# A hybrid block on one Trainium2 core: the band of the local first scores by a TensorE product instead of by VectorE

## The chip, the cores and the metric

The kernel is one program on one core of a Trainium2 chip. Time is device microseconds (us) from launch to end on that core. Before the change three runs gave 568.0, 569.43 and 571.01 us; the median is 569.43 us.

## The reference, cut to what matters

Input is 4 sequences of 512 tokens with 128 channels. Four layers follow each other, each with a layer norm ahead of it and a residual sum behind it: a Haar wavelet mixing ("a"), a mixture of 8 experts with 2 chosen, an attention ("c"), and the same mixture again. The change lies in the attention, of 16 heads with 8 channels:

```
attn = einsum('bhnd,bhmd->bhnm', q, k) * scale
band = abs(idx[:, None] - idx[None, :]) <= 128
local_out  = softmax(where(band, attn, -inf)) @ v
topk_out   = softmax(q . k of the 128 chosen tokens) @ their v
global_out = softmax(q . k of the first 64 tokens) @ their v
out = (local_out + topk_out + global_out) / 3
```

Each of the three softmaxes needs its own maximum for each query. The local one is taken over the band alone: a query block of 128 sees its own key block and half of each neighbour, cut along a diagonal.

## The kernel before, in words

The attention works in 16 groups (NG), each of 4 heads of one sequence. Scores are computed twice. The first scores (`p1`, TensorE) lie with queries on partitions and serve only to find the maxima (`maximum`, VectorE, called DVE below); the maxima are written beside the queries (QST), transposed with them (`transpose_again`), and so are subtracted within the second product. The second scores (`p2`, TensorE) lie with keys on partitions, ScalarE (ACT) takes their exponential into PT (line 1117), and `pv` (TensorE, lines 1935, 1938, 1941) multiplies it by the values.

A group has 22 first-score units (UNITS_Q): for each of 4 heads 4 local ones, a query block each, over 2 key blocks at the edges (256 columns) or 3 in the middle (384 columns); 4 "top" ones over the 128 chosen keys (line 1889), and 2 "global" ones for head pairs (line 1892), both of 512 columns. A local unit is one float16 matmul (line 1884). DVE then runs one instruction that adds the float32 mask BANDQ (0 or -1e30) to the scores, writes the sum to a scratch tile (JUNK, which is XN_a or XN_c) and takes the maximum (line 1460); the trace shows it as CUSTOM_DVE_ANT_0 and a short DVE_READ_ACCUMULATOR2_ANT. The first scores go round 3 PSUM banks: unit v waits until the maximum of unit v-3 is done (`max_done`).

The second scores have 22 units (UNITS) too. Their mask is already a product: TensorE multiplies the identity IDB by the bfloat16 mask BANDK into the bank (lines 1907 and 1910), and the score matmul adds to it (line 1912).

The order is fixed. TensorE's loop goes over groups g and second-score units u; beside each it does the first-score units that `scored_beside` gives, of the group after the next in time (LEAD is 8 units ahead), and at fixed u other work: `transpose_qk` of group g+2 at u=0, `gather_kv` of g+2 at u=13 (lines 1861, 1865: chosen keys and values by one-hot products), `transpose_again` at u=20, and parts of the mixture. The order of the units within a group is `q_order`: globals at places 2 and 5, tops at 8, 11, 14, 17.

Keys reach the matmuls over SyncE's DMA queue (SP). `spread` copies the local keys of a group from KALL to a set of zero-padded tiles (lines 552 and 554, six transfers, the last on line 554) behind ACT's copies on lines 960 and 963; TensorE waits for them (`keys_in`) at the group's first unit. `spread_top` copies the chosen keys (line 560, four transfers) behind DVE's lines 1442 and 1443; TensorE waits for them (`top_keys_in`) at the group's first top unit. The key tiles are of three sets that take turns: KZB, KZC, and the set QS, VS, PR, HXT.

Ahead of the loop stands a prologue (148 to 170 us) that computes the first scores of group 0 and four units of group 1 between the tail of the early mixture (lines 1346, 1347) and the choice of the top tokens.

Of the kernel before, what the change touches and what calls it, by code (L numbers as in the profile page):

```python
# [20 lines left out]
ALU = mybir.AluOpType  # L21
# [3 lines left out]
P = 128  # L25
B, L, D = 4, 512, 128
T = L // P
# [21 lines left out]
GPAIR = 2  # L49
UNITS_Q = HG * (T + 1) + HG // GPAIR  # L50
GLOBAL_W, TOP_W = HG * T, HG * T + HG // GPAIR
UNITS = HG * T + HG + HG // 2
# [26 lines left out]
def key_range(t):  # L79

    return max(t - 1, 0), min(t + 1, T - 1) + 1


def q_order():

    local = [divmod(w, T) for w in range(GLOBAL_W)]
    order = {w: (GPAIR * n, T + 1) for n, w in enumerate((2, 5))} | {w: (i, T) for i, w in enumerate((8, 11, 14, 17))}
    return [order[w] if w in order else local.pop(0) for w in range(UNITS_Q)]


def q_unit(g, w):

    if g >= 2:
        return Q_ORDER[w]
    if w < GLOBAL_W:
        return divmod(w, T)
    if w < TOP_W:
        return GPAIR * (w - GLOBAL_W), T + 1
    return w - TOP_W, T
# [161 lines left out]
def build(nc, x, w_qv, w_out, haar, haar_inv, chan, rows, w_gate, w1, w2, w_qkv, w_s, w_o,  # L261
          ident, band_q, band_k, tri, iota, tie, kshift, out):
    ctx = ExitStack()
    with ctx:
# [87 lines left out]
        VSEL = [sb(f"VSEL{n}", [P, HG, SLOT]) for n in range(3)]  # L352
        JUNK = [XN[n][:, :, :].rearrange("p t d -> p (t d)") for n in "ac"]
        PT = [sb(f"PT{n}", [P, L]) for n in range(PT_RING)]
# [831 lines left out]
        def _(dve):  # L1186
# [260 lines left out]
            def maximum(g, w):  # L1447
# [5 lines left out]
                dve.wait_ge(S["p1_done"], v + 1)  # L1453
                if t < T:
                    lo, hi = key_range(t)
                    n, off = (hi - lo) * P, (lo - t + 1) * P
                    if v >= 2:

                        dve.wait_ge(S["max_done"], v - 1)
                    nc.vector.tensor_tensor_reduce(  # L1460
                        out=JUNK[v % 2][:, 0:n], in0=P1_BANK[v % SCORE_RING][:, 0:n], in1=BANDQ[:, off:off + n],
                        scale=1.0, scalar=OFF, op0=ALU.add, op1=ALU.max,
                        accum_out=qst[:, t, h, SHIFT + LOCAL:SHIFT + LOCAL + 1]).then_inc(S["max_done"], 1)
                elif t == T:
# [200 lines left out]
        def _(pe):  # L1665
# [203 lines left out]
            def p1(g, w):  # L1869
# [8 lines left out]
                if t < T:  # L1878
                    if w == 0:

                        pe.wait_ge(S["misc_free"], free("qk", g) + 1)
                        pe.wait_ge(KEYS_IN[g % 2], spread_done(g))
                    lo, hi = key_range(t)
                    last = mm(bank[:, 0:(hi - lo) * P], q[:, t * P:(t + 1) * P], k[:, lo * P:hi * P], start=True, stop=True)  # L1884
                elif t == T:
# [346 lines left out]
```

## Time and profile before

| | us |
|---|---|
| median of three runs | 569.43 |
| span of the profiled execution, first to last instruction | 567.5 |
| TensorE (PE) busy | 497.0 |
| DVE busy | 390.0 |
| ScalarE (ACT) busy | 350.9 |
| GpSimd (POOL) busy | 311.3 |
| loop over the groups | about 170 to 485 |

The profile gives the profiled execution's span, not its launch time; the median lies 1.9 us above that span. PE's busy time counts overlapping matmuls once but includes the drain of each, so that it overstates how full the array is. Neighbouring starts tell what an instruction really costs its engine when it doesn't wait.

### The profile page before, as it was taken

The numbers are of one execution on the slowest core, as the hardware profiler recorded it, in microseconds if no ns is written. First come the engines' busy times: TensorE is split into PE (matmuls) and PEld (weight loads), VectorE is DVE, ScalarE is ACT, GpSimd is POOL, SyncE is SP. The second block draws the span as 40 slices with busy tenths as digits, with TensorE's granted clock in tenths as the row PEclk, the third lists the DMA queues.
The fourth block names the chain that finished last, engine by engine and source line by source line (L and its number), as shares of the span: only waits on it lengthen the run. The fifth ranks groups of instructions, "written<-read, shape, count | busy, mean of one in ns | idle before, by whom it ended". The sixth has DMA issues, their size and how long they took to land.

```text
span 567.5 us, 13117 instructions
## 1 busy us (share of the span) xinstructions
PE 497.0 (88%) x4267; PEld 307.3 (54%) x4267; DVE 390.0 (69%) x1400; ACT 350.9 (62%) x835; POOL 311.3 (55%) x464
## 2 busy tenths in 40 slices
PE   7999899886767999999899989899987878789886
PEld 4477676676434445545455545445544422668664
DVE  4777876468886698899878897777975650235325
ACT  6587555786208676667567668566664455567653
POOL 3411165456499976493199967897075051354340
PEclk9999999998989999999999999999999697999999
DMA  7996011764210000000000000010001005356506
GB/s 229 360 362 228 2 42 56 255 206 156 64 29 14 3 14 14 14 4 15 12 9 9 15 12 14 27 30 20 12 4 45 12 34 183 125 183 195 163 15 185
DMA packets 47539, 47.78 MB, mean 84 GB/s; under 512 B 10323, under 2 KB 39129, under 8 KB 47472
## 3 DMA queue, kind: packets, MB, share of 16 engines
q1 hardware_dynamic: 44464, 41.37, 23.2%
q0 software_dynamic: 3008, 5.58, 3.1%
q8 instruction: 34, 0.56, 0.4%
q14 instruction: 33, 0.27, 0.1%
HBM read 11.32 MB, written 19.48 MB: 54 GB/s over the span
## 4 chain that ended last, share of the span: by engine, by line
PE 58%; DVE 17%; issue 9%; ACT 7%; DMA 3%; POOL 3%; another core or an unknown queue 2%; SPq 1%; DVEq 0%; ACTq 0%; POOLq 0%
PE BANK L1836 5%; PE BANK L1935 5%; PE BANK L1912 4%; PE BANK L1804 4%; PE BANK L1792 4%; PE BANK L1884 4%; PE BANK L2022 4%; PE BANK L1941 2%; PE BANK L1938 2%; PE BANK L2160 2%; PE BANK L1741 2%; PE BANK L1907 2%; POOL OH L725 2%; DVE XN_c L1460 2%
## 5 line engine op out<-in xcount | busy, mean ns | idle before, releaser
L1117 ACT ACTIVATE PT<-BANK 128x256 f32<-128x256 f32 (+2 forms) x352 | 158.1, 493 | 108.5 <-PE BANK L1912 75.1
L725 POOL TENSOR_SCALAR OH<-IOTA,POS 128x128 bf16<-128x128 bf16 x240 | 140.1, 604 | 4.3 <-DVE OH L1580 3.2
L1460 DVE CUSTOM_DVE_ANT_0 XN_a<-BANK,BANDQ 128x256 f32<-128x256 f32 (+1 forms) x128 | 56.7, 443 | 25.6 <-PE BANK L1884 15.6
L1460 DVE CUSTOM_DVE_ANT_0 XN_c<-BANK,BANDQ 128x384 f32<-128x384 f32 (+1 forms) x128 | 67.9, 530 | 9.3 <-PE BANK L1884 5.5
L733 POOL TENSOR_TENSOR SUM<-NRM 128x128 f32<-128x128 f32 x16 | 7.3, 456 | 104.5 <-DVE NRM L1481 104.5
L1465 DVE TENSOR_REDUCE QST<-BANK 128x4 f16<-128x512 f32 x64 | 44.2, 694 | 16.8 <-PE BANK L1889 12.7
L1935 PE MATMUL BANK<-PT,V 128*32 128x256 f32 (+1 forms) x512 | 49.1, 456 | 0.7 <-issue 0.3
L757 POOL DMA_INDIRECT yt_late<-QKV,IDY_late x31 | 30.4, 979 | 32.7 <-DVE QKV L1338 25.2
L1836 PE MATMUL BANK<-XNT_ALL,W 128*128 128x512 f32 x96 | 45.3, 596 | 0.0
L934 ACT ACTIVATE PT<-BANK 128x512 f32<-128x512 f32 x48 | 27.6, 598 | 22.3 <-PE BANK L1836 20.4
L1907 PE MATMUL BANK<-BANDK,IDB 128*128 128x256 bf16 x128 | 36.0, 282 | 5.7 <-issue 3.5
L2022 PEld LDWEIGHTS BANK<-W,PT 128*128 128x128 f32 x256 | 30.8, 192 | 7.4 <-issue 5.7
L757 POOL DMA_INDIRECT yt_early<-QKV,IDY_early x23 | 22.6, 981 | 19.2 <-ACT QKV L990 10.6
L2022 PE MATMUL BANK<-W,PT 128*128 128x128 f32 x256 | 31.5, 276 | 0.7 <-ACT PT L941 0.7
L1910 PE MATMUL BANK<-BANDK,IDB 128*128 128x128 bf16 x128 | 28.6, 225 | 3.9 <-ACT PT L1117 2.1
L1910 PEld LDWEIGHTS BANK<-BANDK,IDB 128*128 128x128 bf16 x128 | 12.5, 98 | 34.7 <-ACT PT L1117 13.9
L746 POOL DMA_INDIRECT xs_late<-QKV,IDX x24 | 23.8, 990 | 7.9 <-issue 7.1
L970 ACT COPY QKV<-BANK 128x128 f32<-128x128 f32 x54 | 14.1, 260 | 19.3 <-PE BANK L1783 11.3
L1468 DVE TENSOR_REDUCE QST<-BANK 128x8 f16<-128x512 f32 x32 | 22.2, 695 | 5.2 <-remote 3.2
L1323 DVE TENSOR_SCALAR IDY_late<-QKV 128x1 uint32<-128x1 f32 x31 | 4.7, 151 | 29.2 <-PE BANK L1804 17.8
L1884 PE MATMUL BANK<-KZC,QT 128*128 128x256 f16 (+1 forms) x80 | 23.8, 300 | 1.0 <-DVE QST L1460 0.9
L1884 PE MATMUL BANK<-KZB,QT 128*128 128x256 f16 (+1 forms) x80 | 23.5, 300 | 1.2 <-DVE QST L1460 1.1
(363 smaller groups left out, 1286.6 us busy)
## 6 DMA issues: line engine op xcount, KB each, us to landing
xs_late<-W SPq DMA_DIRECT2D x1, 6984.0 KB, 38.4
xs_early<-W SPq DMA_DIRECT2D x1, 4680.0 KB, 19.6
KZB<-W SPq DMA_DIRECT2D x16, 256.0 KB
KZC<-W SPq DMA_DIRECT2D x15, 256.0 KB
PT<-W SPq DMA_DIRECT2D x11, 256.0 KB
QKV<-xs_late SPq DMA_DIRECT2D x31, 72.0 KB
W<-w SPq DMA_DIRECT2D x2, 1024.0 KB, 8.5
QKV<-xs_early SPq DMA_DIRECT2D x23, 72.0 KB
```

The lines of the kernel that those rows point to most:

```text
L725: last = nc.gpsimd.tensor_scalar(OH[g % 2][:, i, t, :], IOTA[:, :], POS[:, t, c:c + 1], None, ALU.is_equal)
L757: nc.gpsimd.indirect_dma_start(YT[w.tag][:, :], bass.IndirectOffsetOnAxis(ap=IDY[w.tag][:, i:i + 1], axis=0), YST[w.tag][slot], None, boun ...
L934: nc.scalar.activation(RELU[u % 4][:, :], UP_BANK[hh][:, :], ACT.Relu).then_inc(s["relu"], 1)
L1117: nc.scalar.activation(PT[u % PT_RING][:, 0:w], P2_BANK[u % SCORE_RING][:, 0:w], ACT.Exp, scale=SCALE).then_inc(S["exp_done"], 1)
L1460: nc.vector.tensor_tensor_reduce(out=JUNK[v % 2][:, 0:n], in0=P1_BANK[v % SCORE_RING][:, 0:n], in1=BANDQ[:, off:off + n], scale=1.0, scala ...
L1465: nc.vector.reduce_max(qst[:, :, h, SHIFT + TOP], P1_BANK[v % SCORE_RING][:, :].rearrange("p (t s) -> p t s", t=T), AX_X).then_inc(S["max_ ...
L1836: mm(UP_BANK[hh][:, :], W1[:, e, hh * P:(hh + 1) * P], XNT_ALL[:, cols(b)], start=True, stop=True).then_inc(s["up"], 1)
L1884: last = mm(bank[:, 0:(hi - lo) * P], q[:, t * P:(t + 1) * P], k[:, lo * P:hi * P], start=True, stop=True)
L1907: mm(edges, IDB[:, :], BANDK[:, :, :], start=True, stop=False, skip_group_check=True)
L1910: mm(bank[:, (q - lo) * P:(q - lo + 1) * P], IDB[:, :], BANDK[:, side, :], start=True, stop=False, skip_group_check=True)
L1935: last = mm(out_n[:, lo * P:hi * P], V32[par][:, r, h, :], pt[:, 0:(hi - lo) * P], start=(r == 0), stop=False, skip_group_check=True)
L2022: last = mm(DOWN_BANK[n % 2][:, t * P:(t + 1) * P], HID_T[n % 2][hh][:, t * P:(t + 1) * P], W2[:, e, hh, :], start=(hh == 0), stop=(hh == ...
```

## The change

Four things change in the attention's first scores.

A local unit first multiplies IDB by both halves of BANDK (256 columns) into the bank, and its score matmuls add to that. DVE's instruction becomes a plain maximum (`reduce_max`) over the bank; BANDQ and JUNK are no longer used there, nor the wait of a maximum on the one two before it.

A head's first and last query blocks (t = 3 and t = 0) share one unit: the mask product fills blocks 0 and 3 of the bank, the last query block's scores (256 columns) go to the left half, the first's to the right half, and one `reduce_max` of 512 columns gives both maxima. The two middle blocks stay units of 384 columns.

So a head has 3 local units instead of 4, and a group 18 units instead of 22; tops stand at places 7, 10, 13, 16.

LEAD (8) and FIRST_LEAD (4) stay, and `scored` spreads the 18 units over the same 22 second-score units.

```diff
-UNITS_Q = HG * (T + 1) + HG // GPAIR
-GLOBAL_W, TOP_W = HG * T, HG * T + HG // GPAIR
+EDGES = 0
+LOCAL_Q = T - 1
+UNITS_Q = HG * (LOCAL_Q + 1) + HG // GPAIR
+GLOBAL_W, TOP_W = HG * LOCAL_Q, HG * LOCAL_Q + HG // GPAIR
...
-    local = [divmod(w, T) for w in range(GLOBAL_W)]
-    order = {w: (GPAIR * n, T + 1) for n, w in enumerate((2, 5))} | {w: (i, T) for i, w in enumerate((8, 11, 14, 17))}
+    local = [divmod(w, LOCAL_Q) for w in range(GLOBAL_W)]
+    order = {w: (GPAIR * n, T + 1) for n, w in enumerate((2, 5))} | {w: (i, T) for i, w in enumerate((7, 10, 13, 16))}
...
-                if t < T:
-                    lo, hi = key_range(t)
-                    n, off = (hi - lo) * P, (lo - t + 1) * P
-                    if v >= 2:
-
-                        dve.wait_ge(S["max_done"], v - 1)
-                    nc.vector.tensor_tensor_reduce(
-                        out=JUNK[v % 2][:, 0:n], in0=P1_BANK[v % SCORE_RING][:, 0:n], in1=BANDQ[:, off:off + n],
-                        scale=1.0, scalar=OFF, op0=ALU.add, op1=ALU.max,
-                        accum_out=qst[:, t, h, SHIFT + LOCAL:SHIFT + LOCAL + 1]).then_inc(S["max_done"], 1)
+                if t == EDGES:
+                    nc.vector.reduce_max(qst[:, ::1 - T, h, SHIFT + LOCAL], P1_BANK[v % SCORE_RING][:, :].rearrange("p (t s) -> p t s", t=2),
+                                         AX_X).then_inc(S["max_done"], 1)
+                elif t < T:
+                    nc.vector.reduce_max(qst[:, t, h, SHIFT + LOCAL:SHIFT + LOCAL + 1], P1_BANK[v % SCORE_RING][:, 0:3 * P],
+                                         AX_X).then_inc(S["max_done"], 1)
...
-                    lo, hi = key_range(t)
-                    last = mm(bank[:, 0:(hi - lo) * P], q[:, t * P:(t + 1) * P], k[:, lo * P:hi * P], start=True, stop=True)
+                    blocks = bank[:, :].rearrange("p (n s) -> p n s", n=T)
+                    mm(blocks[:, 0:T:T - 1, :] if t == EDGES else blocks[:, 0:T - 1:2, :], IDB[:, :], BANDK[:, :, :],
+                       start=True, stop=False, skip_group_check=True)
+                    if t == EDGES:
+                        mm(bank[:, 0:2 * P], q[:, (T - 1) * P:T * P], k[:, (T - 2) * P:T * P],
+                           start=False, stop=False, skip_group_check=True)
+                        last = mm(bank[:, 2 * P:4 * P], q[:, 0:P], k[:, 0:2 * P], start=False, stop=True, skip_group_check=True)
+                    else:
+                        last = mm(bank[:, 0:3 * P], q[:, t * P:(t + 1) * P], k[:, (t - 1) * P:(t + 2) * P],
+                                  start=False, stop=True, skip_group_check=True)
```

The spreading moves units past other work. The first place is TensorE around `gather_kv`, where a group's first unit waits for its keys. Before (1884 are first scores, 1907, 1910 and 1912 second scores, 1935 `pv`, 1861 and 1865 `gather_kv`):

```order
L1884 MATMUL BANK<-KZB,QT 128x256 [waits max_done]
L1935 MATMUL BANK<-PT,V 32x384 [waits exp_done]
L1935 MATMUL BANK<-PT,V 32x384 x3
L1861 MATMUL BANK<-OH,KST 32x128 [waits misc_free,onehot,stack_v]
L1861 MATMUL BANK<-OH,KST 32x128 x15
L1865 MATMUL BANK<-V,OH 128x24 x16
L1910 MATMUL BANK<-BANDK,IDB 128x128 [waits exp_done]
L1912 MATMUL BANK<-QT,PR 128x256
L1884 MATMUL BANK<-KZC,QT 128x256 [waits keys_in1,misc_free,max_done]
```

The same place now (1881 is the mask product of a first-score unit, 1884, 1886 and 1888 its scores, 1912, 1915 and 1917 second scores, 1940 `pv`, 1858 and 1862 `gather_kv`):

```order
L1915 MATMUL BANK<-BANDK,IDB 128x128 [waits exp_done]
L1917 MATMUL BANK<-QT,KZC 128x256
L1881 MATMUL BANK<-BANDK,IDB 128x2x128 [waits keys_in0,misc_free,max_done]
L1884 MATMUL BANK<-KZB,QT 128x256
L1886 MATMUL BANK<-KZB,QT 128x256
L1940 MATMUL BANK<-PT,V 32x384 [waits exp_done]
L1940 MATMUL BANK<-PT,V 32x384 x3
L1858 MATMUL BANK<-OH,KST 32x128 [waits misc_free,onehot,stack_v]
L1858 MATMUL BANK<-OH,KST 32x128 x15
L1862 MATMUL BANK<-V,OH 128x24 x16
```

The unit that waits for a new group's local keys stood behind `pv`, `gather_kv` and one second-score unit; it now stands ahead of all three.

The second place is TensorE at the end of a group, where the first top unit waits for its keys. Before (1938 is `pv` of the top scores):

```order
L1884 MATMUL BANK<-KZC,QT 128x384 [waits max_done]
L1938 MATMUL BANK<-PT,VSEL 32x512 [waits exp_done]
L1938 MATMUL BANK<-PT,VSEL 32x512 x3
L1910 MATMUL BANK<-BANDK,IDB 128x128 [waits exp_done,misc_free]
L1912 MATMUL BANK<-QT,KZB 128x256
L1889 MATMUL BANK<-KZC,QT 128x128 [waits top_keys_in1,max_done]
```

Now (1894 is the top unit, 1943 the same `pv`):

```order
L1922 MATMUL BANK<-QT,KZC 128x512 [waits exp_done]
L1894 MATMUL BANK<-KZB,QT 128x128 [waits top_keys_in0,max_done]
L1894 MATMUL BANK<-KZB,QT 128x128 x3
L1943 MATMUL BANK<-PT,VSEL 32x512 [waits exp_done]
L1943 MATMUL BANK<-PT,VSEL 32x512 x3
L1915 MATMUL BANK<-BANDK,IDB 128x128 [waits exp_done,misc_free]
L1917 MATMUL BANK<-QT,QS 128x256
```

The first top unit has moved ahead of `pv` and of the next group's first second-score unit.

## Rows read from the trace of the kernel before

**Rows 1.** The page's busy times, and its chain that ended last, by engine.

```profile
PE 497.0 (88%) x4267; PEld 307.3 (54%) x4267; DVE 390.0 (69%) x1400; ACT 350.9 (62%) x835; POOL 311.3 (55%) x464
...
PE 58%; DVE 17%; issue 9%; ACT 7%; DMA 3%; POOL 3%; another core or an unknown queue 2%; SPq 1%; DVEq 0%; ACTq 0%; POOLq 0%
```

**Rows 2.** Busy time per stretch: us, PE, PEld, DVE, ACT, POOL, granted clock, DMA, GB/s.

```profile
200.00:225.00 25.00, 23.80 (x261) 13.11 (x259) 22.66 (x71) 16.91 (x41) 16.70 (x30) 1.00 0.07 15
...
300.00:325.00 25.00, 24.36 (x274) 13.47 (x277) 20.00 (x71) 17.11 (x42) 23.83 (x38) 1.00 0.05 11
...
sum 270.00, PE 245.93 PEld 134.32 DVE 217.54 ACT 179.82 POOL 189.01; mean PE 20.49 PEld 11.19 DVE 18.13 ACT 14.99 POOL 15.75
```

**Rows 3.** The chain of waits in 170 to 440 us, by line.

```profile
by line: issue 11.3%; PE BANK L1935 8.9%; PE BANK L1912 6.8%; PE BANK L1884 6.6%; POOL OH L725 3.4%; PE BANK L1938 3.3%; PE BANK L1941 3.2%; PE BANK L1889 2.9%; PE BANK L1819 2.9%; PE BANK L1907 2.8%; PE BANK L1915 2.6%; DVE XN_c L1460 2.5%
```

**Rows 4.** The chain piece by piece, 216 to 222 us: start us, us, what.

```profile
218.76 0.16 PE BANK L1884
218.93 0.11 PE BANK L1907
219.03 0.16 PE BANK L1912
219.20 0.11 PE BANK L1884
```

**Rows 5.** Timeline at 300 us: start us, us, engine, line, operation.

```profile
299.80 0.69 DVE L1465 TENSOR_REDUCE QST<-BANK 128x4 f16<-128x512 f32 x1
...
300.40 0.41 DVE L1460 CUSTOM_DVE_ANT_0 XN_a<-BANK,BANDQ 128x256 f32<-128x256 f32 x1
```

**Rows 6.** The timeline at 302 us, DVE.

```profile
302.17 0.55 DVE L1460 CUSTOM_DVE_ANT_0 XN_a<-BANK,BANDQ 128x384 f32<-128x384 f32 x1
...
302.65 0.42 DVE L1460 CUSTOM_DVE_ANT_0 XN_c<-BANK,BANDQ 128x256 f32<-128x256 f32 x1
```

**Rows 7.** The timeline at 225 us, DVE: two units of 256 columns in a row.

```profile
225.34 0.42 DVE L1460 CUSTOM_DVE_ANT_0 XN_c<-BANK,BANDQ 128x256 f32<-128x256 f32 x1
225.69 0.09 DVE L1460 DVE_READ_ACCUMULATOR2_ANT QST<- 128x1 f16 x1
225.69 0.42 DVE L1460 CUSTOM_DVE_ANT_0 XN_a<-BANK,BANDQ 128x256 f32<-128x256 f32 x1
```

**Rows 8.** The timeline around a group's first unit at 319 us.

```profile
316.66 0.59 SPq L554 DMA_DIRECT2D PR<-KALL  x1
...
317.75 0.85 PE L1935 MATMUL BANK<-PT,V 128*32 128x384 f32 x8
...
318.42 0.41 PE L1861 MATMUL BANK<-OH,KST 128*32 128x128 bf16 x16
...
319.67 0.27 PE L1884 MATMUL BANK<-QS,QT 128*128 128x256 f16 x1 [0.17 <-DMA PR<-KALL]
```

**Rows 9.** The timeline at the same place of another group, 220 to 224 us.

```profile
220.63 0.59 SPq L554 DMA_DIRECT2D KZB<-KALL  x1
...
222.52 0.85 PE L1935 MATMUL BANK<-PT,V 128*32 128x384 f32 x8
```

**Rows 10.** DMA issues in 170 to 440 us: tiles, queue, count, size, median us to landing.

```profile
KZC<-KALL SPq DMA_DIRECT2D x10, 4.0 KB, 1.7
...
PR<-KALL SPq DMA_DIRECT2D x5, 4.0 KB, 2.9
```

**Rows 11.** Timeline: a top spread at 340 us, and a wait for one at 382 us.

```profile
340.14 0.25 DVE L1443 TENSOR_REDUCE VSEL<-BANK 128x32 f32<-128x96 f32 x1
...
343.78 1.06 PE L1938 MATMUL BANK<-PT,VSEL 128*32 128x512 f32 x8
...
375.47 0.25 DVE L1443 TENSOR_REDUCE VSEL<-BANK 128x32 f32<-128x96 f32 x1
...
377.57 0.59 SPq L560 DMA_DIRECT2D HXT<-KALL  x1
...
381.67 0.38 PE L1889 MATMUL BANK<-QS,QT 128*128 128x128 f16 x4 [1.01 <-DMA HXT<-KALL]
```

**Rows 12.** The timeline in the prologue, DVE.

```profile
161.80 0.53 DVE L1460 CUSTOM_DVE_ANT_0 XN_a<-BANK,BANDQ 128x384 f32<-128x384 f32 x1
...
165.18 1.34 DVE L1468 TENSOR_REDUCE QST<-BANK 128x8 f16<-128x512 f32 x2 [0.42 <-PE BANK L1892]
```

**Rows 13.** The chain at 282 us.

```profile
282.56 9.27 POOL OH L725 x16
```

More of the change, by code:

```diff
@@ L95, in q_unit @@
     if w < GLOBAL_W:
-        return divmod(w, T)
+        return divmod(w, LOCAL_Q)
     if w < TOP_W:
@@ L352, in build @@
         VSEL = [sb(f"VSEL{n}", [P, HG, SLOT]) for n in range(3)]
-        JUNK = [XN[n][:, :, :].rearrange("p t d -> p (t d)") for n in "ac"]
         PT = [sb(f"PT{n}", [P, L]) for n in range(PT_RING)]
```

## Prediction, made before the changed kernel ran

> **What bounds the kernel now.** I read the page's busy times and chain first, then busy time by stretch, then the chain piece by piece in the loop over groups, since the change touches nothing outside it but the prologue. TensorE (PE) is busy 88% of the span and DVE 69%, and of the chain that ended last PE holds 58% and DVE 17% [rows 1]. In the loop both are nearly full: 24.36 us of 25 for PE with DVE at 20.00 in one stretch, 23.80 and 22.66 in another [rows 2]. Over 170 to 440 us PE shows no work for 270.0 - 245.9 = 24.1 us, 1.6 us per group of some 18 us [rows 2]. That is an upper limit to what PE can take without being longer, if the gaps stood in the right place.
>
> The piecewise chain shows what a PE-bound stretch looks like: products follow each other without a gap, each at its pitch, 0.11 us for 256 columns and 0.16 us for 384 at the full granted clock [rows 4, 2]. The durations that the timeline gives for the same instructions (0.27 and more [rows 8]) include the drain and must not be summed. Where DVE bounds, the chain runs through the maxima of line 1460 and PE's next unit waits for a bank. So two prices are needed for each edit, and the share of time in which each engine is the one that ends last.
>
> **Term 1, the mask products on PE.** Each local unit gains one product of 256 columns. A head has 3 units, so 12 in a group and 15 x 12 = 180 in the loop (group 0 is scored in the prologue); at 0.107 us, between the rounded 0.11 and what 0.16 us for 384 columns gives for 256, they cost 180 x 0.107 = 19.3 us of PE [rows 4]. The score matmuls keep their columns, 2 x 256 + 2 x 384 per head, so nothing comes back. The identity must be loaded for each mask, and the loads hide beside the product ahead of them, as they do for the second scores' masks [rows 4].
>
> How much of the 19.3 us lies on the path? The masks stand in the very places of line 1884, so I take the share in which those places are on the chain now. Line 1884 holds 6.6% of the chain in 170 to 440 us, 17.8 us [rows 3]; all its matmuls there are some 120 x 0.107 + 120 x 0.16 = 32 us at their pitch [rows 4], so 56% of them are on the chain. A check: line 1907, the same product for the second scores, holds 2.8% = 7.6 us of 112 x 0.107 = 12 us, 63%. At 56% the masks cost 10.8 us. The rest hides behind DVE's maxima, behind ACT, and behind such stretches as the 9.27 us in which GpSimd's one-hots hold the chain [rows 13]. Ends of this term: 19.3 us if that cover is gone, and 0.3 of it, 5.8 us, if the 24.1 us of gaps take most of it.
>
> **Term 2, DVE's maxima.** Again the pitch counts. A unit of 256 columns takes 225.69 - 225.34 = 0.35 us with its read of the accumulator [rows 7], one of 384 takes 302.65 - 302.17 = 0.48 us [rows 6]. A plain maximum over 512 columns takes 300.40 - 299.80 = 0.60 us [rows 5]. One over 384 columns is not in the trace. Its bounds are 0.35 us (the 256-column unit) and 0.60 us (the 512-column maximum); I take 0.47, the 0.60 less the 0.13 us by which 384 and 256 columns differ. A head then costs 0.60 + 2 x 0.47 = 1.54 us instead of 2 x 0.35 + 2 x 0.48 = 1.66 us. The saving is 0.12 us per head, about 7 us over the 60 heads of the loop, of which DVE's 17% of the chain [rows 1] leave 1.2 us. With 0.60 for the middle units it would be a loss of 0.14 us per head, 8 us of DVE, 1.4 us on the path; with 0.35 a gain of 0.36 per head, 22 us of DVE and 3.7 us on the path. The wait of a maximum on the one two before it also goes; in rows 7 the second unit starts at the same 225.69 us as the first's read, so it costs nothing now.
>
> The Trainium skill ("VectorE: DVE Perf Modes", section "Rules for kernel authors") speaks against this edit: it calls `tensor_reduce` the slowest VectorE operation and advises restructuring it away. The rows don't bear that out here: the 512-column reduction at 0.60 us [rows 5] is cheaper than the two 256-column units it replaces, 0.70 us [rows 7]. By the rule term 2 would be at or above zero, and the sum 1.2 us or more higher.
>
> **Term 3, a group's first unit and its local keys.** The unit that waits for `keys_in` moves ahead of a `pv` and `gather_kv`, so it is wanted at about the start of that `pv` instead of 1.9 us later (317.75 against 319.67 us [rows 8]). When it waits, `pv`, `gather_kv` and the second-score units queue behind it, and ACT waits for those. The last transfer of the spread lands a median 1.7 us after its issue for the sets KZB and KZC and 2.9 us for the third set [rows 10]. For the third set: 316.66 + 2.9 = 319.6 us, 1.8 us after the 317.75 us at which it would be wanted [rows 8]. For the others: 220.63 + 1.7 = 222.3 us, 0.2 us ahead of 222.52 [rows 9]. Between the spread and this place PE gets some 5 new masks, 0.55 us, which come off the wait. That leaves 1.2 us for a third-set group; the same sum over its five groups gives 1.3, 0, 1.2, 1.2 and 0.3 us, 4.0 us, and near zero for the other eight. With the share of term 1, 56%, it is 2.2 us. Ends: 0, and 9 us if the masks give no relief and every group waits.
>
> **Term 4, the first top unit and its keys.** It moves ahead of a `pv` of 1.0 us. The four transfers are issued within 2.1 us behind DVE's VSEL instruction (375.47 to 377.57 us) [rows 11] and land about 1.9 us later, so 4.0 us after VSEL; it will be wanted at 343.78 - 340.14 = 3.6 us [rows 11] plus about 0.3 us of new masks. That is 0.1 us late per group in the tight groups; I take 0.5 us in all. One group already waits 1.01 us for such a transfer, which took 381.6 - 377.6 = 4 us [rows 11], and would wait a microsecond longer. Ends: 0 and 5 us.
>
> **Term 5, the prologue.** After the residual sums DVE does six local units before the first global one, 161.80 to 165.18 us, 3.4 us [rows 12]; of 12 local units instead of 16, only two are left there, 0.95 us, so 2.4 us go. Ahead of it the same counts of units now hold more edge units: 3 to 6 cost 0.5 us more and 7 to 9 cost 0.35 us more, and PE, which at this place has a slower pace than DVE, gives back some 0.3 us. Net -1.2 us; ends -2.4 and 0.
>
> **The sum.** 10.8 - 1.2 + 2.2 + 0.5 - 1.2 = +11.1 us on the profiled execution's 567.5 us span, 578.6 us. The median of the runs shown is 1.9 us above that span, 569.4 us, so I predict 580.5 us, 1.9% slower.
>
> **The rivals.**
> *DVE is the bound, faster.* If PE's gaps swallow the masks and DVE, with 22.66 us busy of 25 [rows 2], sets the pace, then the whole 7 us of DVE and the 1.2 us of the prologue come off: 561 us. Fewer units also mean fewer handovers. It decides once the 1.28 us of masks per group fit in the 1.6 us of gaps per group. Against it: the gaps are waits for ACT and DMA too, and in the stretches of rows 4 there is none for tens of products on end. Chance 7%.
> *The masks hide and DVE's saving too.* Terms 1 and 3 near zero, the rest small: 567 to 571 us. Against it stands the share of line 1884 on the chain. Chance 8%.
> *PE becomes the bound throughout.* All 19.3 us on the path, with the key waits in full (4.0 and 1 us), less the prologue: 569.4 + 23 = 592 us. For it: once PE has 1.28 us more per group, the places where DVE or ACT ended last by little go over to PE, so the share of 56% must grow. Against it: GpSimd, ACT and instruction stalls still hold some stretches. Chance 12%.
> *The change doesn't do what it says,* in that the edge unit's strided mask or the plain maximum of 384 columns costs more than its columns (0.60 us for the middle units): +2.6 us on the forecast, 583 us, inside its range and counted with it.
>
> **How the numbers follow.** Forecast 73% (its own range 574 to 588 us: term 1 between 5.8 us and 16 us, the key terms between 0 and 5 us), PE throughout 12%, no change 8%, DVE 7%. A measurement of this kernel can tell about 0.5%, 2.8 us, from no change. Of the forecast's 73% some 2 fall below that. Slower 84%, within 8%, faster 8%. The range for 8 in 10 leaves out the DVE rival, the fast part of the no-change case and the far end of the PE rival: 571 to 590 us.
>
> **What would show it.** PE's busy time in the loop up by some 20 us, with a line of 192 products of 256 columns at a pitch of 0.11 us in stretches without gaps. DVE's line 1460 gone, reductions of 384 columns at a pitch near 0.47 us. DVE more idle, waiting for PE. PE waiting for DMA at the first unit of third-set groups. Groups 0.7 to 1 us longer, except those held by GpSimd. The prologue about 1 us shorter. It is wrong if the loop's groups keep their length although PE's stream is longer (the gaps took it), or if PE's waits for DVE's maxima fall by more than the masks add.

## The result, and the profile after

The changed kernel takes 586.94 us, median of four runs (583.5 to 590.98), against 570.22 us for the kernel before beside it: ratio 1.0286, 95% interval 1.0217 to 1.0354. In a later batch, on another chip, it was 559.82 against 542.31 us, ratio 1.031 [1.0277, 1.0344]. The prediction was 580.5 us, +1.9%, with a range of 571 to 590 us. Its sign and its range hold; +2.9 to +3.1% is 5 to 6 us more than it said. The four runs lie in two pairs, 583.5 and 583.67 us and 590.22 and 590.98 us, so that two of them are above the range. One execution of the kernel before (929.92 us) and one of e2 (1222.99 us) were in a slow state and are in no ratio.

The profiled execution is of the lower pair: 583.67 us, with a span of 581.8 us. First its busy times and its chain by engine, which answer to [rows 1].

```profile
PE 510.5 (88%) x4455; PEld 324.6 (56%) x4455; DVE 381.4 (66%) x1080; ACT 354.7 (61%) x835; POOL 311.6 (54%) x464
...
PE 55%; DVE 15%; issue 8%; ACT 7%; DMA 5%; SPq 4%; another core or an unknown queue 2%; POOL 2%; DVEq 0%; POOLq 0%; ACTq 0%
```

PE has 188 instructions more in the records and 13.5 us more of busy time, DVE 320 fewer and 8.6 us less. If the masks alone had made the chain longer, PE's share would have grown. It fell from 58% to 55%, and DMA with the queue that SP issues (SPq) rose from 4% to 9%. That is the first sign that something besides the masks costs time. TensorE's clock is not it: in 170 to 460 us the mean granted clock is 0.98 before and 0.99 after.

The groups of instructions in 170 to 456 us show both edits. The columns are: line, engine, operation, tiles, shapes, count; busy us and mean ns of one; idle us just before them, by what ended it.

```profile
L1459 DVE TENSOR_REDUCE QST<-BANK 128x1 f16<-128x384 f32 x114 | 63.0, 554 | 34.1 <-PE BANK L1888 33.2
L1881 PE MATMUL BANK<-BANDK,IDB 128*128 128x256 bf16 x173 | 47.2, 273 | 3.0 <-DVE QST L1456 1.2 <-DMA PR<-KALL 0.8 <-DVE QST L1459 0.6
L1456 DVE TENSOR_REDUCE QST<-BANK 128x2 f16<-128x512 f32 x58 | 40.2, 693 | 20.6 <-PE BANK L1886 16.0 <-remote 3.4 <-issue 0.7
```

DVE's maxima of line 1459 sit idle 33.2 us for PE's scores of line 1888, and those of line 1456 16.0 us. PE waits 1.8 us for DVE before its masks. So in the loop DVE waits for PE's local scores far more than PE waits for the maxima: what is taken off DVE buys little, as the prediction had it. (Line 1888 is the score product of a middle unit, 1456 and 1459 are the maxima of an edge pair and of a middle unit.)

The chain of waits shows the masks where PE is the bound (start us, us, what), in the place of [rows 4]:

```profile
238.33 0.16 PE BANK L1917
238.50 0.11 PE BANK L1881
238.60 0.16 PE BANK L1888
238.77 0.11 PE BANK L1912
```

The mask of line 1881 stands between the two products that were neighbours before, and adds its whole pitch of 0.11 us. Eleven microseconds later the same chain looks like this:

```profile
249.37 0.18 DVE VSEL L1444
...
249.56 0.51 SPq L561
...
251.38 1.79 DMA KZC<-KALL
...
253.31 0.38 PE BANK L1894 x4
253.69 0.99 PE BANK L1943 x8
```

Here nothing of PE's sets the time: the path runs from DVE's gather of the chosen keys (VSEL) through four issues of SP, the last at 251.38 us, to the landing of the last transfer, and the top unit (line 1894) starts behind it at 253.31 us. PE itself is idle for 0.78 us of it. `pv` (line 1943), which stood ahead of this unit before, now stands behind it. The 3.9 us that this path takes are the 4.0 us of term 4. What the prediction put too low is how often it ends last. The first local unit has the same kind of chain, from ACT's copy of the keys through six issues, the last at 324.45 us:

```profile
320.06 0.53 ACT KALL L961
...
321.37 0.51 SPq L553
...
324.45 1.76 DMA PR<-KALL
...
326.34 0.27 PE BANK L1881
```

Copy to product takes 6.3 us. Read the two kinds of entry together. An SPq or DMA piece on the chain says that the product behind it started on a landing; the chain then follows the transfer back to its issue and its producer. The list of waits gives only the part in which PE was visibly idle (in 170 to 450 us; us in total, times, longest):

```profile
PE BANK L1881 <- DMA PR<-KALL: 0.8, 3, 0.4
PE BANK L1894 <- DMA KZC<-KALL: 0.8, 1, 0.8
PE BANK L1894 <- DMA HXT<-KALL: 0.8, 1, 0.8
PE BANK L1894 <- DMA KZB<-KALL: 0.7, 1, 0.7
...
```

With two more entries of 0.2 us that is 3.5 us, whereas the pieces of SPq and DMA on the chain in the same window, summed, are 34.8 us (11.4 us before). The two numbers answer different questions: the first is PE's idle time, the second is how much of the elapsed time is set by that path rather than by work of an engine.

### The profile page after: what moved, and what is told of

The parts are those of the page before. It is cut to its first block, busy times and chain, and to the rows that moved or that the text cites. A ratio compares the mean times of both kernels' runs of the same rounds, so it can differ in the third digit from the quotient of the medians.

```text
span 581.8 us, 12963 instructions
## 1 busy us (share of the span) xinstructions
PE 510.5 (88%) x4455; PEld 324.6 (56%) x4455; DVE 381.4 (66%) x1080; ACT 354.7 (61%) x835; POOL 311.6 (54%) x464
## 4 chain that ended last, share of the span: by engine, by line
PE 55%; DVE 15%; issue 8%; ACT 7%; DMA 5%; SPq 4%; another core or an unknown queue 2%; POOL 2%; DVEq 0%; POOLq 0%; ACTq 0%
PE BANK L1940 5%; PE BANK L1833 4%; PE BANK L1789 4%; PE BANK L1801 4%; PE BANK L1917 3%; PE BANK L1946 3%; PE BANK L1943 2%; PE BANK L1881 2%; PE BANK L2027 2%; SPq L553 2%; PE BANK L1888 2%; PE BANK L1894 2%; PE BANK L2165 2%; ACT PT L1118 2%
## 5 line engine op out<-in xcount | busy, mean ns | idle before, releaser
L1118 ACT ACTIVATE PT<-BANK 128x256 f32<-128x256 f32 (+2 forms) x352 | 161.3, 489 | 115.7 <-PE BANK L1917 84.4
L1459 DVE TENSOR_REDUCE QST<-BANK 128x1 f16<-128x384 f32 x128 | 70.4, 554 | 34.8 <-PE BANK L1888 33.5
L1456 DVE TENSOR_REDUCE QST<-BANK 128x2 f16<-128x512 f32 x64 | 44.4, 693 | 25.2 <-PE BANK L1886 20.6
L1881 PE MATMUL BANK<-BANDK,IDB 128*128 128x256 bf16 x192 | 53.1, 276 | 3.7 <-DVE QST L1456 1.4
L1912 PE MATMUL BANK<-BANDK,IDB 128*128 128x256 bf16 x128 | 35.4, 277 | 4.7 <-ACT PT L1118 2.9
L1105 ACT COPY QT<-BANK 128x512 f16<-128x512 f16 x16 | 9.5, 597 | 27.3 <-PE BANK L1816 26.3
L1833 PEld LDWEIGHTS BANK<-XNT_ALL,W 128*128 128x128 f32 x96 | 16.7, 191 | 14.2 <-issue 12.4
```

The costliest lines, as they stand in the source:

```text
L1118: nc.scalar.activation(PT[u % PT_RING][:, 0:w], P2_BANK[u % SCORE_RING][:, 0:w], ACT.Exp, scale=SCALE).then_inc(S["exp_done"], 1)
L1456: nc.vector.reduce_max(qst[:, ::1 - T, h, SHIFT + LOCAL], P1_BANK[v % SCORE_RING][:, :].rearrange("p (t s) -> p t s", t=2), AX_X).then_inc ...
L1459: nc.vector.reduce_max(qst[:, t, h, SHIFT + LOCAL:SHIFT + LOCAL + 1], P1_BANK[v % SCORE_RING][:, 0:3 * P], AX_X).then_inc(S["max_done"], 1)
L1833: mm(UP_BANK[hh][:, :], W1[:, e, hh * P:(hh + 1) * P], XNT_ALL[:, cols(b)], start=True, stop=True).then_inc(s["up"], 1)
L1881: mm(blocks[:, 0:T:T - 1, :] if t == EDGES else blocks[:, 0:T - 1:2, :], IDB[:, :], BANDK[:, :, :], start=True, stop=False, skip_group_che ...
L1912: mm(edges, IDB[:, :], BANDK[:, :, :], start=True, stop=False, skip_group_check=True)
```

## The experiments

Each ratio is to the kernel before, run in turn with it on the same chip, with a 95% interval. A difference in us behind a ratio is the ratio less one, times the time before; it can differ by 1 us from the difference of the medians (for e5 7.9 against 6.8 us). The open point after the first result was why +16 us and not +11. The texts name three theories: A, the mask products' time on PE is the loss and the moved waits are a minor part, as the prediction had it; B, the moved waits are the larger part; C, the coarser maxima on DVE are the loss. Three parts can be had apart: the products that add the masks, DVE's plain maxima, and the places in the order (LEAD and the place of the first top unit). The texts quoted are those written before each run.

**The masks alone, the places alone, and the change without masks.**

e2_masks_only puts the product into the kernel before and leaves its order and its maxima:

```diff
+ if t < T - 1:
+     mm(blocks[:, 0:T - 1:2, :] if t else bank[:, 2 * P:4 * P], IDB, BANDK, start=True, stop=False)
- last = mm(bank[:, 0:(hi - lo) * P], q[...], k[...], start=True, stop=True)
+     last = mm(bank[:, 0:(hi - lo) * P], q[...], k[...], start=False, stop=True)
```

> The kernel before, with the same 12 mask products of 256 columns per group on TensorE as the changed kernel has (the middle units get the real mask, the first query block's unit writes its product to the unused half of the bank), and VectorE, the units and their order as before. Theory A: 8 to 14 us slower than before, 578 to 584 us. Theory B: 2 to 5 us slower. Theory C: within 3 us of before.

Measured: 575.86 against 567.96 us, 1.0152 [1.0121, 1.0183], +8.6 us (6.9 to 10.4). Of 19.3 us of products 45% are on the path (36 to 54%), where the prediction took 56%. Its chain by engine:

```profile
PE 67%; DVE 14%; issue 7%; ACT 6%; another core or an unknown queue 3%; DMA 2%; POOL 0%; SPq 0%; DVEq 0%; POOLq 0%; ACTq 0%
```

PE's share goes from 58% to 67%, the picture that the whole change did not show. In 170 to 450 us no SPq or DMA piece is on its chain at all. The time is at the low end of theory A's 8 to 14 us.

e5_before_lead9 adds and removes no work. It puts every first-score unit of the loop one unit earlier, and with them the two that wait for keys: the first local unit and the first top unit stand ahead of a `pv` as after. It doesn't separate these two from the rest of the shift:

```diff
- LEAD = 8
+ LEAD = 9
```

> The kernel before with LEAD 9 instead of 8: nothing is added, but a group's first unit stands ahead of pv and gather_kv and its first top unit ahead of the pv of the top scores, as in the changed kernel. Theory A: 1 to 5 us slower than before (the waits without the cover of the masks). Theory B: 8 us or more slower, 578 us or more. Theory C: within 2 us of before.

Measured: 574.73 us, 1.0139 [1.0105, 1.0172], +7.9 us. Terms 3 and 4 had 2.7 us for this, theory A 1 to 5 us and theory B 8 us or more, so B is the nearer one here. Its chain at a first top unit, which the kernel before passes at the same time of its span without a piece of SPq or DMA:

```profile
206.36 0.26 DVE VSEL L1443
...
206.64 0.51 SPq L560
...
208.46 1.80 DMA HXT<-KALL
...
210.39 0.38 PE BANK L1889 x4
210.78 1.00 PE BANK L1938 x8
```

PE was idle 0.49 us before 210.39. The list of waits has these entries for transfers, against 1.2 us before (the 1.01 us of [rows 11] and the 0.17 us of [rows 8]):

```profile
PE BANK L1889 <- DMA HXT<-KALL: 1.5, 2, 1.1
PE BANK L1889 <- DMA KZC<-KALL: 1.4, 2, 0.9
PE BANK L1889 <- DMA KZB<-KALL: 1.4, 1, 1.4
PE BANK L1884 <- DMA KZB<-KALL: 1.0, 2, 0.8
PE BANK L1884 <- DMA KZC<-KALL: 1.0, 1, 1.0
PE BANK L1917 <- DMA HXT<-KALL: 0.7, 1, 0.7
PE BANK L1884 <- DMA PR<-KALL: 0.6, 1, 0.6
```

They add up to 7.6 us. The 0.7 us at line 1917 is no wait for keys: it falls at 444 us into a pause in which DVE is idle for 2.69 us too. Against that, two waits of the first local unit, 0.81 and 0.80 us, stand in the list under DVE (NRM); e9 below shows that they are waits for keys. Together that is 8.5 us, 7.3 us more than before.

e3_no_mask is the changed kernel without its mask products:

```diff
- mm(blocks[...], IDB, BANDK, start=True, stop=False)
- mm(bank[:, 0:2 * P], ..., start=False, stop=False)
+ mm(bank[:, 0:2 * P], ..., start=True, stop=True)
```

> The changed kernel without the mask products in the first scores (the band is left out of the local maxima; all else as changed). What is left is the new order and VectorE's plain, paired maxima. Theory A: 9 to 14 us faster than the changed kernel, 570 to 576 us. Theory B: 577 to 583 us, since the waits stay (they even lose the masks' cover). Theory C: within 3 us of the changed kernel.

Measured: 574.47 us, 1.0113 [1.0081, 1.0145], +6.4 us with not one product more on PE. It differs from e5 by DVE's maxima and the pairing of the edge blocks, with 18 units in place of 22, and the two ratios by -0.26%, 1.5 us, with intervals that overlap: term 2's -1.2 us fits. Masks (e2) and the rest (e3) multiply to 1.0267, against 1.0286 and 1.031 for the whole.

e1_lead7 is the changed kernel with one number altered. It puts every first-score unit of the loop one unit later, the local keys' and the top keys' first use back behind a `pv` among them:

```diff
- LEAD = 8
+ LEAD = 7
```

> The changed kernel with LEAD 7 instead of 8: the first unit of a group and its first top unit go back behind gather_kv and behind the pv of the top scores. Theory A (the mask products' time on TensorE is the loss, the moved waits a minor part): about 2 to 4 us faster than the changed kernel, so about 579 to 584 us, still 2% slower than before. Theory B (the moved waits are the larger part): 8 us or more faster, 571 to 576 us. Theory C (coarser maxima on VectorE are the loss): no change from the changed kernel, 583 to 590 us.

Measured: 577.9 us, 1.0177 [1.0146, 1.0208]. The masks stay, a full point goes; the 577.9 us lie between the ranges of theory A (579 to 584) and B (571 to 576). No SPq or DMA piece is left on its chain in 170 to 450 us, and its page reads like that of the masks alone:

```profile
PE 70%; DVE 12%; issue 8%; ACT 6%; DMA 1%; another core or an unknown queue 1%; SPq 1%; POOL 0%; DVEq 0%; ACTq 0%; POOLq 0%
```

**Which of the two places, and can the gain be had?** These ran on another chip (before: 567.29 us).

e8_top_early exchanges the first top unit with the local unit ahead of it and moves nothing else. e9_first_early takes LEAD 9, so that every first-score unit stands one earlier, the first local one among them, and puts the first top unit back to where it was. Both are made from the kernel before:

```diff
- order = ... enumerate((8, 11, 14, 17))
+ order = ... enumerate((7, 11, 14, 17))      # e8, LEAD 8
+ order = ... enumerate((9, 11, 14, 17))      # e9, with LEAD 9
```

> The kernel before with the first top unit at place 7 instead of 8 of its group: it stands ahead of the pv of the top scores, the group's first unit stays behind gather_kv. If the top keys' place is what cost LEAD 9 its 1.4%: 1.0 to 1.4% slower than before. If it is the local keys' place: within 0.4%. My prediction for the changed kernel had it at 0.5 us.

> The kernel before with LEAD 9 and the first top unit at place 9: the group's first unit stands ahead of pv and gather_kv, the first top unit stays behind the pv of the top scores. If the local keys' place is what cost LEAD 9 its 1.4%: 1.0 to 1.4% slower than before. If it is the top keys' place: within 0.4%. My prediction for the changed kernel had it at 2.2 us.

Measured: e8 570.42 us, 1.0062 [1.0042, 1.0083], +3.5 us, where term 4 had 0.5; e9 572.0 us, 1.0076 [1.0043, 1.0109], +4.3 us, where term 3 had 2.2. Together 1.38%, which is e5's 1.39%: two separate costs that add. Neither text had this: each gave 1.0 to 1.4% to one of the places. The runs of e9 lie in two clusters (568.1 to 571.0 and 573.0 to 576.5 us), and the profiled one, 575.61 us, is of the upper one, so its 4.3 us are less sure than e8's.

The list of waits of e9 has only these for transfers:

```profile
PE BANK L1889 <- DMA KZB<-KALL: 1.0, 1, 1.0
PE BANK L1884 <- DMA KZC<-KALL: 1.0, 1, 1.0
PE BANK L1884 <- DMA PR<-KALL: 0.5, 1, 0.5
```

The first is at the top unit, so 1.5 us at the local unit seem to stand for a cost of 4.3 us. But four more waits of 0.80 to 0.84 us, 3.3 us in all, end at a group's first local unit and are put down to DVE's normalization of an earlier group (NRM). One of them, with the last issue of that group's keys:

```profile
319.22 0.59 SPq L554 DMA_DIRECT2D PR<-KALL  x1
...
320.43 0.56 DVE L1481 TENSOR_TENSOR NRM<-BANK,RD 128x384 f32<-128x384 f32 x1
...
321.12 0.27 PE L1884 MATMUL BANK<-QS,QT 128*128 128x256 f16 x1 [0.82 <-DVE NRM L1481]
```

NRM ends at 320.99 us, and the transfer, issued at 319.22 us and landed a median 1.8 us after its issue, comes at 321.0 us: the two fall together. The unit does not need NRM. Of the bank that NRM frees it waits only for the use at u=0 (`transpose_qk`), which was over before PE transposed into that bank at 318.33 us what NRM reads. From the last issue to the unit it is 1.90 us here, 1.89 us in the changed kernel (324.45 to 326.34 us), where the list does name the transfer, and 1.85 to 1.89 us in the other three. So the first local units of e9 wait 4.7 us for keys, 4.6 us more than before, and that is its 4.3 us. That the rest of the shift costs nothing is inferred from this match, not tested by itself.

Term 3 gave the waits to the third set (4.0 us in five groups) and "near zero" to the others. In e9 three groups of the third set wait 2.1 us, and three of the others 2.65 us.

The 2.9 us to landing that term 3 took for the third set [rows 10] come from something else. A DMA view of the kernel before, 316.6 to 319.7 us (first row: packets, MB, share of 16 engines; second: count, size, median us to landing), against the same transfer in e5, 319 to 321 us, where the view has no row of kind "instruction":

```profile
q8 instruction: 1, 0.02, 1.8%
...
PR<-KALL SPq DMA_DIRECT2D x1, 4.0 KB, 2.9
```

```profile
PR<-KALL SPq DMA_DIRECT2D x1, 4.0 KB, 1.8
```

The packet of kind "instruction" is one of 16 KB and ran from 317.09 to 317.96 us, while the keys were on their way. All fourteen traces say the same. Of 644 key transfers in 170 to 450 us whose landing is told, 95 took over 2.2 us, and every one of the 95 overlaps such a packet of 8 or 16 KB; of the 549 others 441 overlap none. The late landings come again at the same transfers of kernels that keep the old order: the two late ones of the third set take 2.9 and 3.2 us before, 2.8 and 3.4 in e8, 2.9 and 3.5 in e7, 2.5 and 3.3 in e10. In e5, e9 and the changed kernel no told last transfer of that set takes over 1.8 us. So the 2.9 us belonged neither to the set nor to chance but to where these packets fell, and where a group's first unit stands earlier they fell elsewhere. In e9 one such packet hit another set: the wait of 0.98 us has a landing of 2.6 us ahead of it.

e6_no_mask_lead7 joins e1 and e3: the changed kernel without masks, with LEAD 7.

> The changed kernel without mask products (the band is left out of the local maxima) and with LEAD 7: only VectorE's paired, plain maxima are left of the change. If the losses add up (masks +1.5%, moved places +1.4%), this equals before within 0.5%, 565 to 570 us, with no DMA wait of TensorE at a group's first unit. If VectorE's coarser units were a loss of their own, it is over 1% slower than before. If the saving of VectorE counted in full (7 us), it would be 561 us.

Measured: 566.45 us, 0.9972 [0.9946, 0.9999]. Against e3's 1.0113 the place alone is worth 1.4% once more. It leaves the mask out, so it is no version to use; it bounds what cheaper maxima with LEAD 7 could bring. The text had 565 to 570 us.

e4_pairs_only is a version with the full computation: LEAD 7, the edge pair masked by a product (one product per head instead of three), the two middle units again by DVE's sum and maximum.

```diff
- mm(blocks[...] , IDB, BANDK, start=True, stop=False)        # every unit
+ if t == EDGES: mm(blocks[:, 0:T:T - 1, :], IDB, BANDK, start=True, stop=False)
- nc.vector.reduce_max(qst[...], P1_BANK[...][:, 0:3 * P], AX_X)
+ nc.vector.tensor_tensor_reduce(out=JUNK[v % 2][:, 0:3 * P], in0=P1_BANK[...][:, 0:3 * P], in1=BANDQ, ...)
```

> A candidate: only a head's first and last blocks are paired and masked by a product; the two middle units have VectorE's sum and maximum in one instruction as before and no product, and LEAD is 7. A third of the mask products (60 in the loop, 6.4 us of TensorE) and nearly all of VectorE's saving are left. If a mask product costs what the masks-only run showed (8.7 us for 180), this is 2 to 3 us slower than before, 0.5%, less 0 to 1.5 us of VectorE's saving: 567 to 571 us. If VectorE's saving counted in full it would be 4 us faster than before.

Measured: 573.22 us, 1.012 [1.0076, 1.0163]. A miss as a version and of its text (567 to 571 us): slower than before, though faster than the change.

**The parts of e4, and the plain maxima by themselves.** This batch ran on a third chip, on which the kernel before takes 542.31 us.

e7_before_lead7 is the kernel before with LEAD 7. e11_pairs_no_mask is e4 without its product.

> The kernel before with LEAD 7: a group's first unit and first top unit one place later than before. If waits for keys are what the place costs, before has 1.2 us of them and this is equal or up to 1 us faster. If a shorter lead costs time of its own (VectorE's maxima are needed sooner by transpose_again), it is 2 us or more slower, and that is a hidden loss in the kernels with LEAD 7.

> The pairs-only kernel (LEAD 7) without its mask product (the first and last blocks' band is left out of the maxima; the middle units keep theirs). If products are dear in proportion, this is 3 to 4 us faster than the pairs-only kernel, about 569 us. If the first products cost more than the rest (TensorE's gaps would have to be where the other masks stand), it is 6 us or more faster, near 566 us. If the middle units' form is what costs, it stays above 570 us.

Measured: e7 545.13 us, 1.0046 [1.0024, 1.0068]; e11 545.16 us, 1.0044 [1.0024, 1.0065]. An earlier place costs, and so does a later one: LEAD 7 is 0.46% worse than 8 where there are no masks; what it waits for was not traced. And pairing the edge blocks without a mask adds nothing to that, so the joint bank is free but brings nothing. From e11 to e4 a third of the products cost 0.76%, where a third of e2's 1.52% would be 0.5%; the two ran on different chips, and the intervals allow it. e1 can now be put together: 1.52 (masks) + 0.46 (LEAD 7) - 0.26 (maxima) = 1.72%, measured 1.77%.

e10_plain_max takes the band out of the kernel before's maxima and leaves the rest:

```diff
- nc.vector.tensor_tensor_reduce(out=JUNK[v % 2][:, 0:n], in0=P1_BANK[...][:, 0:n], in1=BANDQ[...], ...)
+ nc.vector.reduce_max(qst[...], P1_BANK[...][:, 0:n], AX_X)
```

> The kernel before, 22 units in their order, with a plain maximum in place of VectorE's sum and maximum (the band is left out of the local maxima, TensorE is untouched). By the pitches in the trace (0.47 to 0.48 us for 384 columns either way) it is within 0.3% of before. If the one-instruction form with its accumulator read costs more than its pitch shows, as 573 us for the pairs-only kernel suggests, it is 0.5 to 1% faster, 562 to 565 us.

Measured: 541.6 us, 0.9983 [0.9958, 1.0008]: -0.9 us, no difference that can be told. Plain maxima are worth next to nothing on the path. e6 against e11 would say -0.7% for the two middle units, on different chips; that disagreement stays open.

e12_after_again is the changed kernel on this chip.

> The changed kernel once more, beside the others, since its four runs lay in two clusters (583.6 and 590.6 us) and the sum of the parts needs its ratio more closely. If the parts add up (masks 1.5%, moved places 1.4%, VectorE's part -0.3%): 2.6% slower than before, 582 us. If 590 us is the rule, there is an interaction of some 7 us that no part shows.

Measured: 559.82 us, 1.031 [1.0277, 1.0344], +16.8 us, where the text had 2.6% if the parts add up. The kernel before has no profile on this chip; e10, 0.9 us from it, stands in. The `pv` products of the global scores, the last of each group (line 1936 in e10, 1946 in e12), show where the difference arises. The two times are the starts of the first, at the end of group 0, and of the last, at the end of group 15:

```profile
L1936 PE MATMUL BANK<-PT,VGZ x128: 592/605/617, 190.8 to 458.4; 128*32 128x512 f32 x128
```

```profile
L1946 PE MATMUL BANK<-PT,VGZ x128: 592/605/617, 191.3 to 477.4; 128*32 128x512 f32 x128
```

These 15 groups grow from 267.6 to 286.1 us, 18.5 us of the 19.1 us between the two spans (538.4 and 557.5 us), and what lies ahead, prologue and group 0, by 0.5 us: the loss is in the loop.

A summary of the chain in 170 to 450 us (SPq and DMA pieces summed from each trace's list of pieces) beside the ratios:

| kernel | SPq + DMA on the chain, us | ratio |
|---|---|---|
| before | 11.4 | 1 |
| e8, top unit early | 15.3 | 1.0062 |
| e9, local unit early | 15.6 | 1.0076 |
| e5, both early | 32.1 | 1.0139 |
| e3, both early, no masks, plain maxima | 42.8 | 1.0113 |
| after | 34.8 (e12: 38.3) | 1.0286 (1.031) |
| e2, masks only | 0 | 1.0152 |
| e1, after with LEAD 7 | 0 | 1.0177 |

The pieces are not a price: e3 has more of them than e5 and is no slower. They tell which kernels are held by the path through SP and which are not. The 15.6 us of e9 are too low, and so to a lesser degree are e5's 32.1: where a wait is put down to NRM, the chain leaves the transfer.

## Why the prediction was right, and which term was not

**The bound, and the direction.** Right. That the size came within 6 us is in part luck: the masks were put 2.2 us too high and the places 5.2 us too low, and the two errors partly cancel. PE ends last in most of the loop, and work moved from DVE to PE makes the kernel slower.

**Term 1, the masks: +10.8 us.** Measured by e2 at +8.6 us (6.9 to 10.4). The pitch of 0.107 us stands in the chain as 0.11. The share on the path was 45%, not 56%: right in kind, a little high. The rival with all 19.3 us on the path is excluded by e2, and so is the one in which the gaps take the masks. (The three chances given for slower, within and faster, 84, 8 and 8%, don't quite follow from the rivals' own: those make 83, 10 and 7%.)

**Term 2, DVE: -1.2 us.** e10 has -0.9 us (-2.3 to +0.4), e3 less e5 -1.5 us. Right. Two maxima of 384 columns in a row take 0.99 us at 0.55 us each, a pitch of 0.44, so the rival in which the middle units cost 0.60 us falls:

```profile
164.10 0.99 DVE L1459 TENSOR_REDUCE QST<-BANK 128x1 f16<-128x384 f32 x2
```

The rule of the Trainium skill ("VectorE: DVE Perf Modes", "Rules for kernel authors") against `tensor_reduce` would have had this term at or above zero; e10 bears out the rows rather than the rule, though its interval just reaches zero.

**Terms 3 and 4, the two places: +2.7 us together. These were mis-sized.** e5 has +7.9 us, e9 and e8 +4.3 and +3.5 us. The mechanism was right: DVE's gather or ACT's copy, then SP's issues in a row, then the landing, with PE's queue held at the unit that needs them. Three steps of the sizing failed.
- Term 4 took "0.1 us late per group in the tight groups" from one group's times (3.6 us against 4.0). The five waits for transfers at line 1889 in e5 are up to 1.4 us long, 4.3 us in all. Groups differ by more than the margin that one of them shows.
- Term 3 took the landing of 2.9 us for a property of the third set and found all its waits there. With the new order that set lands after 1.8 us, and the units of the other two sets, for which it had near zero, account for more than half: 2.65 us of e9's 4.7.
- Both were multiplied by the share of term 1, 56%. A wait for a transfer is not like one more product: what would have filled it, `pv`, is queued behind it. The waits for keys grew by 7.3 us in e5, 4.6 us in e9 and 1.9 us in e8, and the costs are 7.9, 4.3 and 3.5 us. The share should have been one.

**"New masks come off the wait."** Half right. At the first local unit of one and the same group PE waits 0.84 us in e3, without masks (at 322.70 us), and 0.22 us after (at 326.34 us): 0.6 us less, where the prediction had 0.55. In all the visible waits are 3.5 us instead of e5's 8.5. But the places cost nearly as much with masks as without: from LEAD 7 to LEAD 8 of the changed kernel the ratio rises by 1.1% (from e1 to the first measurement) or 1.3% (to e12), and without masks, from e6 to e3, by 1.4%. Relief that shows in PE's idle time did not show in the time. A likely reason, argued and not tested, is that masks delay DVE's maxima and so its gather too, so that the transfers start later.

**Term 5, the prologue: -1.2 us.** Right up to the end of the prologue, and mostly lost just behind it. On the third chip, in e10 and after (e12), ACT's copy of group 0's transposed queries, with which the prologue ends, and the first exponential of the loop:

```profile
166.21 0.58 ACT L1104 COPY QT<-BANK 128x512 f16<-128x512 f16 x1 [25.35 <-PE BANK L1814]
167.30 1.35 ACT L1117 ACTIVATE PT<-BANK 128x256 f32<-128x256 f32 x3 [0.51 <-PE BANK L1907]
```

```profile
165.18 0.58 ACT L1105 COPY QT<-BANK 128x512 f16<-128x512 f16 x1 [24.32 <-PE BANK L1816]
166.96 1.26 ACT L1118 ACTIVATE PT<-BANK 128x256 f32<-128x256 f32 x3 [1.20 <-PE BANK L1917]
```

The copy comes 1.03 us earlier (in e7, with the old maxima, it is at 166.26 us), the exponential 0.34 us: between the two PE does the first units of group 1, which now carry masks, and ACT waits 1.20 us instead of 0.51. On the other chips the start of the loop can't be compared that closely: the first exponential comes at 170.5 us before and 172.7 us after, but at 168.2 us in e8, whose prologue is that of the kernel before.

PE's clock takes no side. In both kernels PE is idle for 3.7 us for DVE in the prologue (to 158.48 us in e10, to 158.85 us in e12) and restarts at a granted clock of 0.50, the lower of its two levels, 1.2 and 2.4 GHz; the stretch of 162 to 164 us, e10 and e12 (columns as in [rows 2]):

```profile
162.00:164.00 2.00, 2.00 (x14) 1.28 (x13) 1.57 (x3) 0.00 (x0) 1.70 (x4) 0.55 0.00 0
```

```profile
162.00:164.00 2.00, 2.00 (x10) 0.93 (x8) 1.40 (x2) 0.00 (x0) 1.66 (x5) 0.50 0.00 0
```

**What is left.** Masks 8.6, places 7.9, DVE -1.5 make 15.0 us or 2.65%, of the 2.86% first measured and the 3.10% of e12. The 0.2 to 0.45 points between lie inside the interval of the first; they lie just outside that of the second (from 2.77%), but the sum has an interval of its own, some 0.45 points either way (from those of e2 and e3). No run settles whether masks and places add more than their sum.

No kernel with the full computation was faster than the one before. The best of them that still masks by a product was e4, at 1.012.

## What to carry to other kernels

On an engine that works in order, a unit that waits for a transfer must have its filler ahead of it: an order in which two such units stand one `pv` earlier cost 0.6 and 0.8%, together nearly as much as 180 extra products of 256 columns. Size such a move by the whole path from the last producer to the landing (4.0 us here) against where each group wants it, count a late transfer in full, and distrust a margin read from one group. Where a landing is late, look for other packets in the same microsecond. Where a wait is put down to an instruction that the code does not wait for, look for a landing at the same moment: in e9 this had hidden 3.3 of 4.7 us. Read a table of positions as part of the change: one number in it (e1) gave back 38% of the loss.

## What the runs showed of the hardware that was not expected

**Chips differ, and in pauses of several engines.** The same kernel takes 542.3 us on the third chip and 567 to 570 us on the others. Its profiles on the slower chips hold waits with no releaser in the profile (remote), several engines at once. Those of the kernel before:

```profile
ACT PT L1117 <- remote: 10.3, 4, 3.9
DVE XN_a L1460 <- remote: 4.2, 1, 4.2
DVE QKV L1382 <- remote: 3.8, 1, 3.8
```

One of them in the timeline of the kernel before:

```profile
438.30 0.60 ACT L1117 ACTIVATE PT<-BANK 128x512 f32<-128x512 f32 x1 [3.94 <-remote]
438.96 0.61 PE L1917 MATMUL BANK<-QT,KZB 128*128 128x512 f16 x1 [3.07 <-issue]
439.00 0.42 DVE L1460 CUSTOM_DVE_ANT_0 XN_a<-BANK,BANDQ 128x256 f32<-128x256 f32 x1 [4.17 <-remote]
```

ACT, PE and DVE stop together for 3 to 4 us and go on within 0.7 us of each other. GpSimd goes on issuing in the same stretch. The profiles of the third chip have no such wait. What causes them was not found; a difference of 1% must be read from ratios on one chip, and a single trace from these chips can carry 4 us at any place that are not the kernel's.

**A small transfer that lands late has a packet of instructions beside it.** The last 4 KB of a group's local keys, from SBUF to SBUF, land 1.7 to 1.8 us after their issue, and in some groups up to 3.5 us after it, at the same transfers on different chips. All 95 late landings (over 2.2 us) of the fourteen traces overlap a packet of 8 or 16 KB on a queue of kind "instruction"; of the others one in five does. That the packet is what delays them is inferred from this; no run moved the packets alone.
